# Small running maxima moved from SBUF into free columns of a PSUM bank, in a fused Perceiver block

## The chip, the core and the metric

The kernel runs on one core of one Trainium2 chip. The metric is the device time of one execution in microseconds (us), shown as the median of three runs. The engines are named as in the profile: PE is TensorE (matrix products), DVE is VectorE, ACT is ScalarE, POOL is GpSimd, SP is SyncE, which only issues DMAs here.

## What is computed

Three layers follow one another on `x` (8 batches, 128 rows, 512 columns), each with a residual add:

```
x = x + xattn(layernorm(x), ctx)   # 8 heads of 64, softmax over 2048 context rows of 384
x = x + attn(layernorm(x))         # causal mask, softmax over axis 1, 512 wide
x = x + ffn(layernorm(x))          # 512 -> 2048 -> 512, relu, hidden rounded to an 8-bit float
```

The change lies in the first layer, the cross attention. For each batch and head it is

```
q = xn @ Wq ; k = ctx @ Wk ; v = ctx @ Wv
attn = softmax(q k^T / 8)  over 2048 context rows
out  = (attn @ v) @ Wo + bo
```

## The kernel before

The cross attention is cut into `SLOTS = 128` slots: 8 batches, 4 quarters of the context (512 rows each), 4 pairs of heads. Slot `s` is head pair `p = s % 4` of unit `i = s // 4`; a unit is one quarter of one batch. Each matrix is kept as a high and a low half-precision part, and a product takes three passes. One step `s` of the pipeline does on PE: the values of slot s+1 into the PSUM bank `v_ps` (`value_tiles`), the keys of slot s into `k_ps` (`key_quarter`), the product of probabilities and values of slot s-5 into `o_ps[s % 2]` (`weighted_values`), and in even steps the scores of slots s-2 and s-1 into `e_ps[0]` and `e_ps[1]` (`scores`). So the work goes in pairs of steps.

The softmax is a running one over the four quarters of a batch. For each slot DVE reduces the scores to a negated maximum for each row and head (`quarter_maximum`). In quarter 0 this goes straight to `run`. In quarters 1 to 3 it goes to `q_max`, and a second instruction (L1535) takes the smaller of `q_max` and the `run` of the quarter before; that is the new `run`. ACT turns `run` into the bias of the exponential (`quarter_bias`, L1176) and computes the exponentials twice, as a half-precision part `p_h` (L1199) and in full as `p_f` (L1201). POOL subtracts the two for the low part `p_l` (L1981). SP turns both parts around by DMA transposes (L595, L598), and `weighted_values` reads them. `gaps` (L1543), once for each pair of slots in quarters 1 to 3, subtracts the old from the new `run`; ACT makes the factor `fade` from it (`fades_of`, L1185), by which DVE scales the accumulated output (`accumulate`, L1562). `GAPS` lists the even slots at which this happens, 48 of them.

Each engine runs its instructions in the order in which they are written, and waits on semaphores. The orders that matter here:

- DVE in an odd step s: the two maxima of slots s-3 and s-2, `accumulate` of slot s-6, the low part of the values of slot s+1 (`v_low`, L1517), `gaps`, the low part of the keys of slot s (`k_low`, L1521). In an even step: `accumulate`, `v_low`, `k_low`. In steps 111 to 126 a `weight_low` (L1580) stands ahead of `gaps`.
- ACT in an odd step: bias of slot s-3, first half of its exponentials, bias of slot s-2, the high part of the values of slot s+1 (`v_high`, L1164), second half of the exponentials, high part of the keys (`k_high`, L1170), `fades_of`.
- PE: `value_tiles` of the next slot waits until `v_low` has emptied `v_ps`, and `key_quarter` until `k_low` has emptied `k_ps`.
- POOL: `p_low` for each slot; once for each unit `ctx_low` (L1971), the low part of the next quarter of the context; late in the loop `weight_high` (L2040) and `add_bias` (L2025), for the later layers.

`weighted_values` fills columns 0 to 258 of its bank; the other columns of `o_ps[1]` are not used in the loop.

Of the kernel before, what the change touches and what calls it, by code (L numbers as in the profile page):

```python
# [4 lines left out]
F32 = mybir.dt.float32  # L5
# [3 lines left out]
ALU = mybir.AluOpType  # L9
ACT = mybir.ActivationFunctionType  # L10
AX = mybir.AxisListType.X

P = 128
# [3 lines left out]
PAIRS = HEADS // 2  # L17
QUARTERS = 4
# [40 lines left out]
def perceiver_kernel(nc, x, ctx_t, xwq, xwk, xwv, xwo, xbo, awq, abq, awk, abk, awv, abv,  # L59
# [6 lines left out]
        ("bq_col", [P, DCH], F32), ("bk_col", [P, DCH], F32), ("b1_col", [P, HC, 1], F32),  # L66
        ("b2_half", [P, D], F16),
        ("stats", [P, B, 6], F32), ("mean_var", [P, B, 2], F32), ("rstd", [P, B], F32), ("exponent", [P, B], F32),
        ("q_max", [P, 2, 2], F32), ("run", [P, 2, PAIRS, 2], F32), ("bias", [P, 2, PAIRS, 2], F32), ("gap", [P, 2, PAIRS, 2], F32),
        ("fade", [P, 2, PAIRS, 2], F32), ("acc", [P, PAIRS, 2, VW], F32), ("o_rec", [P, PAIRS, 2, 1], F32), ("o_sum", [P, 2, DH], F32),  # L70
        ("o_f", [P, 2, DH], F32),
        ("ones", [P, P], F32), ("bq_half", [P, DCH, 2], F16), ("bk_half", [P, DCH, 2], F16), ("bias_prod", [P, DCH], F32),
# [89 lines left out]
    assert t_halves_end <= halves_end  # L162

    (o_all, ident, causal, bo_row, bv_row, b2_row, bq_col, bk_col, b1_col, b2_half, stats, mean_var, rstd, exponent,
     q_max, run, bias, gap, fade, acc, o_rec, o_sum, o_f,
     ones, bq_half, bk_half, bias_prod, u_col, w_col, w_half, s_col, c_sum, c_col,
     shift) = keep.values()
    q_h, q_l = queries.values()
# [31 lines left out]
    with ExitStack() as ctx:  # L200
        def psum(name, shape):
            return ctx.enter_context(nc.psum_tensor(name, shape, F32))

        def sem(name):
            return ctx.enter_context(nc.semaphore(name))

        v_ps, k_ps = psum("v_ps", [P, 512]), psum("k_ps", [P, 512])
        e_ps = [psum("e_ps0", [P, 2, 512]), psum("e_ps1", [P, 2, 512])]
        o_ps = [psum("o_ps0", [P, 512]), psum("o_ps1", [P, 512])]

        kv_bank = [v_ps, k_ps]
        t_bank = [e_ps[0][:, 0, :], e_ps[0][:, 1, :], e_ps[1][:, 0, :], e_ps[1][:, 1, :]]
        r_bank = o_ps
        q_bank = [v_ps, o_ps[0], k_ps, o_ps[1]] + o_ps + o_ps

        const_ready = sem("const_ready")
# [36 lines left out]
        e_maxed = sem("e_maxed")  # L253
        bias_ready = sem("bias_ready")
        q_maxed = sem("q_maxed")
        gap_ready = sem("gap_ready")
# [86 lines left out]
        def unit_of(s):  # L343
            return s // PAIRS, s % PAIRS
# [49 lines left out]
        GAPS = [s for s in range(0, SLOTS, 2) if s // PAIRS % QUARTERS]  # L394

        def gaps_at(s):
            return GAPS.index(s)
# [275 lines left out]
        def _(pe):  # L673
# [78 lines left out]
            def weighted_values(s):  # L752

                i, p = unit_of(s)
                landed = 16 * (s // T_RING) + 16
                pe.wait_ge(pt_h_landed[s % T_RING], landed)
                pe.wait_ge(pt_l_landed[s % T_RING], landed)

                pe.wait_ge(v_split, PAIRS * i + PAIRS)
                if s >= 2:  # L760
                    pe.wait_ge(acc_ready, s - 1)
                elif s == 0:
                    pe.wait_ge(v_ones, 1)
                    pe.wait_ge(q_split, 8)
                acc_bank = o_ps[s % 2]
                for h in range(2):
                    at = h * VW
                    for j in range(JT):
                        pe.matmul(acc_bank[:, at:at + SUM_AT + 1], pt_h[:, s % T_RING, h * JT + j, :],  # L769
                                  v[:, i % V_RING, j, 2 * p + h, 0:SUM_AT + 1],  # L770
                                  start=(j == 0 and h == 0), stop=False, skip_group_check=True)
                        mm = pe.matmul(acc_bank[:, at + DH:at + SUM_AT + 1], pt_l[:, s % T_RING, h * JT + j, :],  # L772
                                       v[:, i % V_RING, j, 2 * p + h, DH:SUM_AT + 1],
                                       start=False, stop=(j == JT - 1), skip_group_check=True)
                mm.then_inc(pv_done, 1)
# [52 lines left out]
            def steady(s):  # L828

                if s + 1 < SLOTS:  # L830
                    value_tiles(s + 1)
                if s < SLOTS:
                    key_quarter(s)
                if 0 <= s - PV_LAG < SLOTS:
                    weighted_values(s - PV_LAG)
                if s % 2 == 0 and 2 <= s <= SLOTS:
                    scores(s - 2)
                    scores(s - 1)
# [199 lines left out]


            weighted_values(SLOTS - PV_LAG)  # L1040
            scores(SLOTS - 2)
            fold(0)
            scores(SLOTS - 1)
            project_out(0)
            for r in range(1, 4):
                weighted_values(SLOTS - PV_LAG + r)
                project_out(r)
# [54 lines left out]
        def _(act):  # L1102
# [76 lines left out]
            def fades_of(s):  # L1179

                i, p = unit_of(s)
                act.wait_ge(gap_ready, gaps_at(s) + 1)
                if i >= 2:
                    act.wait_ge(acc_ready, s - 2 * PAIRS + 2)
                act.activation(fade[:, i % 2, p:p + 2, :], gap[:, i % 2, p:p + 2, :], ACT.Exp, scale=EXP_SCALE)\  # L1185
                    .then_inc(fade_ready, 1)
# [190 lines left out]
            quarter_bias(SLOTS - 1)  # L1377
            exps(SLOTS - 1, 0)
            fades_of(SLOTS - 2)
            exps(SLOTS - 1, 1)  # L1380
            for r in range(3):
# [80 lines left out]
        def _(dve):  # L1462
# [60 lines left out]
            def quarter_maximum(s):  # L1523

                i, p = unit_of(s)
                dve.wait_ge(e_filled, s + 1)
                if i >= 2:
                    dve.wait_ge(bias_ready, s - 2 * PAIRS + 1)
                if i % QUARTERS == 0:
                    dve.tensor_reduce(run[:, i % 2, p, :], e_ps[s % 2][:, :, :], AX, ALU.max, negate=True).then_inc(e_maxed, 1)  # L1530
                    return
                dve.tensor_reduce(q_max[:, s % 2, :], e_ps[s % 2][:, :, :], AX, ALU.max, negate=True).then_inc(q_maxed, 1)  # L1532
                dve.wait_ge(q_maxed, PAIRS * (i - 1 - i // QUARTERS) + p + 1)
                dve.wait_ge(e_maxed, s - PAIRS + 1)
                dve.tensor_tensor(run[:, i % 2, p, :], q_max[:, s % 2, :], run[:, 1 - i % 2, p, :], ALU.min).then_inc(e_maxed, 1)  # L1535

            def gaps(s):

                i, p = unit_of(s)
                dve.wait_ge(e_maxed, s + 2)  # L1540
                if gaps_at(s) >= 4:
                    dve.wait_ge(fade_ready, gaps_at(s) - 3)
                dve.tensor_tensor(gap[:, i % 2, p:p + 2, :], run[:, i % 2, p:p + 2, :], run[:, 1 - i % 2, p:p + 2, :],  # L1543
                                  ALU.subtract).then_inc(gap_ready, 1)

            def accumulate(s):

# [591 lines left out]
```

## Time and profile before

| | |
|---|---|
| median of three runs | 966.65 us (965.09, 966.65, 969.07) |
| the profiled execution | 967.87 us, span from first to last instruction 965.8 us |
| PE | 912.1 us busy, 94% of the span |
| DVE | 642.5 us, 67% |
| ACT | 596.9 us, 62% |
| POOL | 508.6 us, 53% |
| chain that ended last | PE 71%, DVE 13%, ACT 7%, issue 3% |

The first columns say how long an engine worked, not what it held up. The chain is followed back from the last instruction, at each step to what released it. The slots take the time from about 40 to 770 us; what comes after is the two later layers, in which PE is busy too. A timeline row gives start, duration, engine, line, operation, output and inputs, and in brackets the idle time before it and what ended that; adjacent instructions of one kind can stand in one row (x3).

### The profile page before, as it was taken

Reading aid. Unit: us, or ns where it says so; the run is one execution under the profiler, and the core shown is the slowest. Engines: PE = TensorE matmul, PEld = TensorE weight load, DVE = VectorE, ACT = ScalarE, POOL = GpSimd, SP = SyncE. Lnnn points to the kernel's source line nnn. Section 1 sums busy time; section 2 is a strip of 40 time slices with the busy share of each in tenths; the row PEclk is TensorE's granted clock in tenths of the full one; section 3 lists DMA queues with packets and bytes.
Section 4 is the critical chain, followed back from the end, with each engine's and each line's share of the span. In section 5 each row is a group of like instructions: output and inputs, shape, how many; then the busy total and the mean of one; then the engine's idle time right before and its main releaser. Section 6 shows DMA issues by size and latency. Waiting matters only on the chain.

```text
span 965.8 us, 17868 instructions
## 1 busy us (share of the span) xinstructions
PE 912.1 (94%) x6354; PEld 459.8 (48%) x6354; DVE 642.5 (67%) x1085; ACT 596.9 (62%) x1126; POOL 508.6 (53%) x394
## 2 busy tenths in 40 slices
PE   7999999999989999999999999999898899999998
PEld 4444445444544544454445444444443455554444
DVE  6546665666666566656665666678777778886634
ACT  4757767767677766777677668666675712326540
POOL 2535566556645755565467556767796586310000
PEclk9999999999999999999999999999899999999999
DMA  9346766756656566655656766987888546134501
GB/s 327 77 88 120 124 131 153 151 120 127 137 121 126 134 139 128 126 137 134 133 142 134 134 130 137 185 198 143 174 148 170 110 68 140 26 108 88 168 19 76
DMA packets 340263, 126.24 MB, mean 131 GB/s; under 512 B 316113, under 2 KB 317905, under 8 KB 340177
## 3 DMA queue, kind: packets, MB, share of 16 engines
q1 hardware_dynamic: 324032, 94.30, 48.8%
q10 hardware_dynamic: 16144, 30.81, 10.4%
q8 instruction: 52, 0.85, 0.4%
q14 instruction: 35, 0.28, 0.1%
HBM read 45.36 MB, written 2.10 MB: 49 GB/s over the span
## 4 chain that ended last, share of the span: by engine, by line
PE 71%; DVE 13%; ACT 7%; issue 3%; POOL 1%; SPq 1%; DMA 1%; ACTq 0%; DVEq 0%; POOLq 0%
PE v_ps L679 21%; PE k_ps L679 20%; PE e_ps L748 7%; PE e_ps L679 7%; DVE run L1535 5%; PE o_ps L769 4%; DVE q_max L1532 4%; PE e_ps L1034 3%; PE o_ps L772 2%; ACT p_h L1199 2%; ACT v L1164 2%; PE o_ps L1027 2%; DVE v L1517 2%; PE e_ps L1027 1%; ACT p_f L1201 1%
## 5 line engine op out<-in xcount | busy, mean ns | idle before, releaser
L1981 POOL TENSOR_TENSOR p_l<-p_f,p_h 128x1024 f16<-128x1024 f32 x128 | 274.4, 2144 | 268.9 <-ACT p_f L1201 266.0
L1199 ACT ACTIVATE p_h<-e_ps,bias 128x512 f16<-128x512 f32 x256 | 176.7, 690 | 6.2 <-issue 4.0
L1201 ACT ACTIVATE p_f<-e_ps,bias 128x512 f32<-128x512 f32 x256 | 177.3, 693 | 0.0
L1521 DVE TENSOR_TENSOR k_l<-k_ps,k_h 128x512 f16<-128x512 f32 x128 | 88.4, 691 | 128.3 <-ACT k_h L1170 128.3
L1517 DVE TENSOR_TENSOR v<-v_ps,v 128x512 f16<-128x512 f32 x127 | 87.9, 692 | 100.7 <-ACT v L1164 100.5
L679 PE MATMUL v_ps<-wv_h,ctx_h 128*128 128x512 f16 (+1 forms) x384 | 103.0, 377 | 30.5 <-DVE v L1517 30.5
L1532 DVE TENSOR_REDUCE q_max<-e_ps 128x2 f32<-128x1024 f32 x96 | 117.2, 1221 | 7.8 <-PE e_ps L748 2.1
L1176 ACT ACTIVATE bias<-run 128x2 f32<-128x2 f32 x128 | 26.0, 203 | 150.6 <-DVE run L1535 127.7
L679 PE MATMUL k_ps<-ctx_h,wk_h 128*128 128x512 f16 x384 | 105.0, 383 | 9.0 <-DVE k_l L1521 8.7
L769 PE MATMUL o_ps<-v,pt_h 128*128 128x129 f16 x1024 | 106.8, 221 | 2.0 <-DMA pt_l<-p_l 2.0
L679 PE MATMUL k_ps<-ctx_h,wk_l 128*128 128x512 f16 x384 | 105.1, 383 | 0.0
L679 PE MATMUL k_ps<-ctx_l,wk_h 128*128 128x512 f16 x384 | 104.8, 382 | 0.0
L772 PE MATMUL o_ps<-v,pt_l 128*128 128x65 f16 x1024 | 103.4, 193 | 0.0
L1971 POOL TENSOR_TENSOR ctx_l<-raw,ctx_h 128x1536 f16<-128x1536 f32 x31 | 96.0, 3098 | 12.3 <-ACT ctx_h L1156 11.7
L679 PE MATMUL v_ps<-wv_l,ctx_h 128*128 128x512 f16 (+1 forms) x384 | 102.5, 376 | 0.0
L679 PE MATMUL v_ps<-wv_h,ctx_l 128*128 128x512 f16 (+1 forms) x384 | 102.5, 376 | 0.0
L769 PEld LDWEIGHTS o_ps<-v,pt_h 128*128 128x128 f16 x1024 | 92.3, 97 | 17.3 <-issue 2.6
L772 PEld LDWEIGHTS o_ps<-v,pt_l 128*128 128x128 f16 x1024 | 90.8, 98 | 15.1 <-issue 0.3
L1164 ACT ACTIVATE v<-v_ps 128x512 f16<-128x512 f32 x127 | 75.6, 596 | 32.3 <-PE v_ps L679 27.8
L1170 ACT ACTIVATE k_h<-k_ps 128x512 f16<-128x512 f32 x128 | 77.1, 603 | 14.9 <-PE k_ps L679 12.7
L1535 DVE TENSOR_TENSOR run<-q_max,run 128x2 f32<-128x2 f32 x96 | 65.6, 683 | 3.3
L679 PEld LDWEIGHTS v_ps<-wv_h,ctx_h 128*128 128x128 f16 x384 | 28.2, 97 | 75.4 <-issue 60.1
(311 smaller groups left out, 1363.2 us busy)
## 6 DMA issues: line engine op xcount, KB each, us to landing
raw<-in_ctx_t ACTq DMA_DIRECT2D x29, 768.0 KB, 5.1
w_raw<-in_w_t SPq DMA_DIRECT2D x32, 256.0 KB, 3.7
pt_h<-p_h SPq DMA_TRANSPOSE x128, 3.2
pt_l<-p_l SPq DMA_TRANSPOSE x128, 3.1
out<-xr SPq DMA_DIRECT2D x7, 256.0 KB, 2.0
x_in<-in_x SPq DMA_DIRECT2D x6, 256.0 KB, 9.4
raw<-in_ctx_t SPq DMA_DIRECT2D x2, 768.0 KB, 9.7
o_all<-in_x ACTq DMA_DIRECT2D x6, 256.0 KB, 4.5
```

The lines of the kernel that those rows point to most:

```text
L679: mm = pe.matmul(acc, a(c), m(c), start=(i == 0), stop=(i == len(todo) - 1))
L769: pe.matmul(acc_bank[:, at:at + SUM_AT + 1], pt_h[:, s % T_RING, h * JT + j, :], v[:, i % V_RING, j, 2 * p + h, 0:SUM_AT + 1], start=(j == ...
L772: mm = pe.matmul(acc_bank[:, at + DH:at + SUM_AT + 1], pt_l[:, s % T_RING, h * JT + j, :], v[:, i % V_RING, j, 2 * p + h, DH:SUM_AT + 1], ...
L1164: act.activation(v_high_part(s), v_source(s), ACT.Copy).then_inc(v_hi, 1)
L1199: act.activation(p_h[:, s % H_RING, h, :], e_ps[s % 2][:, h, :], ACT.Exp, scale=EXP_SCALE, bias=bias[:, i % 2, p, h:h + 1]).then_inc(p_hi, 1)
L1201: act.activation(p_f[:, s % F_RING, h, :], e_ps[s % 2][:, h, :], ACT.Exp, scale=EXP_SCALE, bias=bias[:, i % 2, p, h:h + 1]).then_inc(p_ful ...
L1517: dve.tensor_tensor(v_low_part(s), v_source(s), v_high_part(s), ALU.subtract).then_inc(v_split, 1)
L1521: dve.tensor_tensor(k_l[:, s % K_RING, :], k_ps[:, :], k_h[:, s % K_RING, :], ALU.subtract).then_inc(k_split, 1)
L1532: dve.tensor_reduce(q_max[:, s % 2, :], e_ps[s % 2][:, :, :], AX, ALU.max, negate=True).then_inc(q_maxed, 1)
L1535: dve.tensor_tensor(run[:, i % 2, p, :], q_max[:, s % 2, :], run[:, 1 - i % 2, p, :], ALU.min).then_inc(e_maxed, 1)
L1971: pool.tensor_tensor(ctx_l[:, i % 2, :, :], raw[:, i % 2, :, :], ctx_h[:, i % 2, :, :], ALU.subtract).then_inc(ctx_split, 1)
L1981: pool.tensor_tensor(p_l[:, s % L_RING, :, :], p_f[:, s % F_RING, :, :], p_h[:, s % H_RING, :, :], ALU.subtract).then_inc(p_split, 1)
```

## The change

`q_max` leaves SBUF. It now lies in columns 384 to 387 of the bank `o_ps[1]`: two columns for the even slot, two for the odd one. A new tile `least` lies in columns 388 to 391. The minimum L1535 now has one input in PSUM (the own maximum) and one in SBUF (`run`). `gaps` becomes two instructions: `least` is the smaller of both slots' own maxima (PSUM) and the old `run` (SBUF), and the gap is `least` (PSUM) minus the old `run` (SBUF). Before, both inputs of the gap were `run`, in SBUF. Since the columns lie in a bank that PE writes, `weighted_values` of the odd slots before a gap also waits for that gap. The lines of the changed kernel are numbered up to 7 higher.

```
-        ("q_max", [P, 2, 2], F32), ("run", ...
+        ("run", ...
...
+        q_max, least = o_ps[1][:, 384:388], o_ps[1][:, 388:392]
...
@@ weighted_values(s), PE
+                if s + 1 in GAPS:
+                    pe.wait_ge(gap_ready, 2 * gaps_at(s + 1) + 2)
...
@@ fades_of(s), ACT
-                act.wait_ge(gap_ready, gaps_at(s) + 1)
+                act.wait_ge(gap_ready, 2 * gaps_at(s) + 2)
...
@@ quarter_maximum(s), DVE
-                dve.tensor_reduce(q_max[:, s % 2, :], e_ps[s % 2][:, :, :], AX, ALU.max, negate=True).then_inc(q_maxed, 1)
-                dve.wait_ge(q_maxed, PAIRS * (i - 1 - i // QUARTERS) + p + 1)
+                own = q_max[:, 2 * (s % 2):2 * (s % 2) + 2]
+                dve.tensor_reduce(own, e_ps[s % 2][:, :, :], AX, ALU.max, negate=True).then_inc(q_maxed, 1)
+                dve.wait_ge(q_maxed, 2 * gaps_at(s - s % 2) + s % 2 + 1)
                 dve.wait_ge(e_maxed, s - PAIRS + 1)
-                dve.tensor_tensor(run[:, i % 2, p, :], q_max[:, s % 2, :], run[:, 1 - i % 2, p, :], ALU.min).then_inc(e_maxed, 1)
+                dve.tensor_tensor(run[:, i % 2, p, :], own, run[:, 1 - i % 2, p, :], ALU.min).then_inc(e_maxed, 1)
...
@@ gaps(s), DVE
-                dve.wait_ge(e_maxed, s + 2)
+                before = run[:, 1 - i % 2, p:p + 2, :].rearrange("p a h -> p (a h)")
+                dve.wait_ge(q_maxed, 2 * gaps_at(s) + 2)
+                dve.tensor_tensor(least, q_max, before, ALU.min).then_inc(gap_ready, 1)
+                dve.wait_ge(gap_ready, 2 * gaps_at(s) + 1)
                 if gaps_at(s) >= 4:
                     dve.wait_ge(fade_ready, gaps_at(s) - 3)
-                dve.tensor_tensor(gap[:, i % 2, p:p + 2, :], run[:, i % 2, p:p + 2, :], run[:, 1 - i % 2, p:p + 2, :],
-                                  ALU.subtract).then_inc(gap_ready, 1)
+                dve.tensor_tensor(gap[:, i % 2, p:p + 2, :].rearrange("p a h -> p (a h)"), least, before, ALU.subtract)\
+                    .then_inc(gap_ready, 1)
```

DVE, one odd step of quarter 1 (the maxima, the values, the gap, the keys), before:

```order
L1532 TENSOR_REDUCE q_max<-e_ps 128x2 [waits bias_ready,e_filled]
L1535 TENSOR_TENSOR run<-q_max,run 128x2 [waits e_maxed,q_maxed]
L1532 TENSOR_REDUCE q_max<-e_ps 128x2 [waits bias_ready,e_filled]
L1535 TENSOR_TENSOR run<-q_max,run 128x2 [waits e_maxed,q_maxed]
L1554 COPY acc<-o_ps 128x2x129 [waits o_ready,pv_done]
L1517 TENSOR_TENSOR v<-v_ps,v 128x8x64 [waits v_hi]
L1543 TENSOR_TENSOR gap<-run 128x4 [waits fade_ready,e_maxed]
L1521 TENSOR_TENSOR k_l<-k_ps,k_h 128x512 [waits k_hi]
```

The same step of DVE in the changed kernel (`o_ps<-e_ps` is the maximum written to its new place, `o_ps<-o_ps,run` is `least`):

```order
L1536 TENSOR_REDUCE o_ps<-e_ps 128x2 [waits bias_ready,e_filled]
L1539 TENSOR_TENSOR run<-o_ps,run 128x2 [waits e_maxed,q_maxed]
L1536 TENSOR_REDUCE o_ps<-e_ps 128x2 [waits bias_ready,e_filled]
L1539 TENSOR_TENSOR run<-o_ps,run 128x2 [waits e_maxed,q_maxed]
L1561 COPY acc<-o_ps 128x2x129 [waits o_ready,pv_done]
L1520 TENSOR_TENSOR v<-v_ps,v 128x8x64 [waits v_hi]
L1546 TENSOR_TENSOR o_ps<-o_ps,run 128x4 [waits q_maxed]
L1550 TENSOR_TENSOR gap<-o_ps,run 128x4 [waits fade_ready,gap_ready]
L1524 TENSOR_TENSOR k_l<-k_ps,k_h 128x512 [waits k_hi]
```

No instruction has moved past another; one is added ahead of the gap, 48 times in all.

PE, the even step after it (keys, then the first instruction of `weighted_values` into `o_ps[1]`), before:

```order
L679 MATMUL k_ps<-ctx_h,wk_h 128x512 [waits k_split,ctx_split]
L679 MATMUL k_ps<-ctx_h,wk_h 128x512 x2
L679 MATMUL k_ps<-ctx_h,wk_l 128x512 x3
L679 MATMUL k_ps<-ctx_l,wk_h 128x512 x3
L769 MATMUL o_ps<-v,pt_h 128x129 [waits v_split,acc_ready,pt_l_landed2,pt_h_landed2]
```

And in the changed kernel:

```order
L680 MATMUL k_ps<-ctx_h,wk_h 128x512 [waits k_split,ctx_split]
L680 MATMUL k_ps<-ctx_h,wk_h 128x512 x2
L680 MATMUL k_ps<-ctx_h,wk_l 128x512 x3
L680 MATMUL k_ps<-ctx_l,wk_h 128x512 x3
L772 MATMUL o_ps<-v,pt_h 128x129 [waits acc_ready,v_split,gap_ready,pt_l_landed2,pt_h_landed2]
```

The wait for `gap_ready` is new. `k_split` in the first row counts the `k_low` that follows this gap on DVE.

## Rows read from the trace of the kernel before

**Rows 1.** Busy time of the page (us, share of the span, instructions).

```profile
PE 912.1 (94%) x6354; PEld 459.8 (48%) x6354; DVE 642.5 (67%) x1085; ACT 596.9 (62%) x1126; POOL 508.6 (53%) x394
```

**Rows 2.** Waits, 80 to 608 us: engine, line, releaser: us, times, longest.

```profile
ACT bias L1176 <- DVE run L1535: 97.3, 35, 3.2
...
PE v_ps L679 <- DVE v L1517: 25.1, 18, 1.4
```

**Rows 3.** Windows, each one pair of slots: busy us by engine, clock, DMA share, GB/s.

```profile
384.31:394.99 10.68, 10.68 (x84) 5.45 (x82) 6.60 (x13) 7.39 (x17) 4.26 (x3) 1.00 0.79 161
394.99:407.21 12.22, 10.82 (x82) 5.46 (x81) 9.04 (x14) 8.65 (x17) 7.35 (x4) 1.00 0.43 96
```

**Rows 4.** Timeline of DVE in the first of these pairs.

```profile
385.18 1.22 DVE L1532 TENSOR_REDUCE q_max<-e_ps 128x2 f32<-128x1024 f32 x1
386.44 0.16 DVE L1535 TENSOR_TENSOR run<-q_max,run 128x2 f32<-128x2 f32 x1
...
388.75 0.69 DVE L1517 TENSOR_TENSOR v<-v_ps,v 128x512 f16<-128x512 f32 x1 [0.25 <-ACT v L1164]
...
390.44 0.69 DVE L1521 TENSOR_TENSOR k_l<-k_ps,k_h 128x512 f16<-128x512 f32 x1 [0.93 <-ACT k_h L1170]
```

**Rows 5.** Timeline of DVE in the second pair.

```profile
397.11 2.44 DVE L1535 TENSOR_TENSOR run<-q_max,run 128x2 f32<-128x2 f32 x1
...
401.70 0.69 DVE L1517 TENSOR_TENSOR v<-v_ps,v 128x512 f16<-128x512 f32 x1 [0.26 <-ACT v L1164]
```

**Rows 6.** Timeline of POOL in the second pair.

```profile
396.44 3.10 POOL L1971 TENSOR_TENSOR ctx_l<-raw,ctx_h 128x1536 f16<-128x1536 f32 x1
```

**Rows 7.** Timeline of PE, the next values in either pair.

```profile
390.31 0.81 PE L679 MATMUL v_ps<-wv_h,ctx_h 128*128 128x512 f16 x3
...
402.54 0.81 PE L679 MATMUL v_ps<-wv_h,ctx_h 128*128 128x512 f16 x3 [1.40 <-DVE v L1517]
```

**Rows 8.** Groups of DVE, 80 to 608 us: xcount, busy us, mean ns, idle before.

```profile
L1535 DVE TENSOR_TENSOR run<-q_max,run 128x2 f32<-128x2 f32 x70 | 52.4, 748 | 2.4
...
L1554 DVE COPY acc<-o_ps 128x258 f32<-128x258 f32 x22 | 9.3, 421 | 0.0
L1543 DVE TENSOR_TENSOR gap<-run 128x4 f32<-128x4 f32 x35 | 5.3, 152 | 0.0
```

**Rows 9.** Single lines, whole span: ns min/median/max, first and last start.

```profile
L1517 DVE TENSOR_TENSOR v<-v_ps,v x127: 684/692/693, 14.1 to 753.1; 128x512 f16<-128x512 f32 x127
```

```profile
L1562 DVE SCALAR_TENSOR_TENSOR acc<-acc,fade,o_ps x192: 334/342/352, 88.1 to 786.4; 128x129 f32<-128x129 f32 x192
```

**Rows 10.** Windows, late in the slots: columns as in Rows 3.

```profile
608.59:755.04 146.45, 133.87 (x962) 66.56 (x961) 109.80 (x163) 95.49 (x184) 108.76 (x70) 0.97 0.82 166
678.00:684.80 6.80, 5.78 (x29) 2.91 (x31) 3.54 (x8) 3.71 (x7) 3.21 (x3) 0.50 0.78 159
729.00:732.60 3.60, 3.19 (x8) 1.17 (x9) 2.06 (x5) 2.91 (x5) 0.45 (x1) 0.53 0.90 206
```

**Rows 11.** Timeline of DVE at the longest late wait.

```profile
673.05 3.23 DVE L1580 SCALAR_TENSOR_TENSOR av_l<-w_in,av_h 128x512 f16<-128x512 f32 x1
676.20 2.07 DVE L1543 TENSOR_TENSOR gap<-run 128x4 f32<-128x4 f32 x1
678.20 0.68 DVE L1521 TENSOR_TENSOR k_l<-k_ps,k_h 128x512 f16<-128x512 f32 x1
```

**Rows 12.** Timeline of POOL at the same place.

```profile
672.63 3.10 POOL L1971 TENSOR_TENSOR ctx_l<-raw,ctx_h 128x1536 f16<-128x1536 f32 x1
```

**Rows 13.** Timeline of PE, the two longest waits for the keys' bank.

```profile
679.02 1.44 PE L679 MATMUL k_ps<-ctx_h,wk_h 128*128 128x512 f16 x3 [3.64 <-DVE k_l L1521]
...
729.40 1.44 PE L679 MATMUL k_ps<-ctx_h,wk_h 128*128 128x512 f16 x3 [3.62 <-DVE k_l L1521]
```

**Rows 14.** Timeline of DVE, last gap of the slots.

```profile
768.20 1.92 DVE L1543 TENSOR_TENSOR gap<-run 128x4 f32<-128x4 f32 x1
```

**Rows 15.** Timeline of PE, first fold of weights after it.

```profile
770.87 1.02 PE L679 MATMUL v_ps<-wo_h,q_h 128*128 128x512 f16 x4 [1.21 <-DVE f_l L1668]
```

More of the change, by code:

```diff
@@ L68, in perceiver_kernel @@
         ("stats", [P, B, 6], F32), ("mean_var", [P, B, 2], F32), ("rstd", [P, B], F32), ("exponent", [P, B], F32),
-        ("q_max", [P, 2, 2], F32), ("run", [P, 2, PAIRS, 2], F32), ("bias", [P, 2, PAIRS, 2], F32), ("gap", [P, 2, PAIRS, 2], F32),
+        ("run", [P, 2, PAIRS, 2], F32), ("bias", [P, 2, PAIRS, 2], F32), ("gap", [P, 2, PAIRS, 2], F32),
         ("fade", [P, 2, PAIRS, 2], F32), ("acc", [P, PAIRS, 2, VW], F32), ("o_rec", [P, PAIRS, 2, 1], F32), ("o_sum", [P, 2, DH], F32),
@@ L164, in perceiver_kernel @@
     (o_all, ident, causal, bo_row, bv_row, b2_row, bq_col, bk_col, b1_col, b2_half, stats, mean_var, rstd, exponent,
-     q_max, run, bias, gap, fade, acc, o_rec, o_sum, o_f,
+     run, bias, gap, fade, acc, o_rec, o_sum, o_f,
      ones, bq_half, bk_half, bias_prod, u_col, w_col, w_half, s_col, c_sum, c_col,
```

## The prediction, made before the changed kernel ran

> **What bounds the kernel now.** I read the busy times first: PE works 94% of the span, some 54 of 965.8 us are left in which it does not [rows 1]. A change that touches no matrix product can win only there, so the next view is the waits, and of them those of PE. From 80 to 608 us PE has one kind of wait only: 18 times for `v_low`, 25.1 us in all, the longest 1.4 us, so all 18 are alike [rows 2]. ACT's 97.3 us of waiting for the running minimum L1535 in the same rows name a suspect, but an idle ACT costs nothing by itself.
>
> Next I cut windows at the starts of successive pairs of scores. A pair without such a wait takes 10.68 us and PE is busy in all of it; one with it takes 12.22 us [rows 3]. The starts of further pairs repeat these two lengths. So 10.67 is the floor that PE sets, and a disturbed pair costs 1.55 us more.
>
> The DVE timelines show where the two differ. In the clean pair the minimum takes 0.16 us [rows 4]. In the disturbed one it takes 2.44 us, for two numbers per partition [rows 5]; it began at 397.11 and ended at 399.55. POOL's `ctx_low` ran from 396.44 to 399.54 [rows 6]. The minimum lasted exactly until POOL was done. The group view says how often: 70 minima from 80 to 608 us take 52.4 us; at 0.16 us each they would take 11.2, so 41.2 us are excess, and 41.2 / 2.28 = 18, the count of PE's waits. The 35 gaps there have a mean of 152 ns: none is held [rows 8].
>
> What is held and what is not? `v_low` reads PSUM and SBUF and writes SBUF; its 127 executions span 684 to 693 ns. `accumulate`, with its large inputs in SBUF and PSUM, spans 334 to 352 ns over 192 [rows 9]. POOL is busy 53% of the time [rows 1], so many of these ran beside it, and none was ever late. The minimum and the gap have both inputs in SBUF, and so has `weight_low`, whose row shows 3.23 us [rows 11]. So what waits for POOL is a DVE instruction with two inputs in SBUF.
>
> How 2.28 us become 1.55: in the clean pair `v_low` ends at 389.44 and PE starts on `v_ps` at 390.31; in the disturbed one `v_low` ends at 402.39 and PE starts 0.15 us later [rows 4, 5, 7]. So a clean pair has 390.31 - 389.44 - 0.15 = 0.72 us of slack, and 2.28 - 0.72 = 1.56.
>
> **The change, part by part.**
>
> *The minima up to 608 us.* With the own maximum in PSUM they have the form of `v_low` and should not wait. 18 disturbed pairs become clean: 18 x 1.55 = 27.9 us.
>
> *What PSUM costs a small instruction.* No row shows DVE writing PSUM, or reading two numbers from it. Lower end: from the reduction of 1024 elements (1.22 us) and the copy of 258 (0.421 us) [rows 4, 8] each element costs (1.22 - 0.42) / 766 = 1.04 ns and a fixed part of 0.15 us is left, no more than a minimum takes today; so no loss. Upper end: a whole `accumulate`, 0.34 us [rows 9], so 0.18 us more per instruction. The near row in kind is the fitted fixed part, and I take 0.02 us more. Even the upper end, on the two reductions and two minima ahead of the second bias, is 4 x 0.18 = 0.72 us, just the slack. So it costs PE nothing at either end; if the cover were gone, the chosen value would cost 48 x 0.08 = 4 us and the upper end 35 us.
>
> The trace has nothing on this path that is dearer for lying in PSUM. Perfetto Trace Analysis, in its section Optimizing Scalar/DVE Operations, in the Trainium skill, speaks against the change: it gives about 125 ns of access overhead for DVE on PSUM against about 60 on SBUF. By that, four accesses on the path would add an estimated 0.26 us per pair, and the sum would still be the same, as that lies inside the slack; no run here shows the figure.
>
> *The added `least`.* One more instruction of 0.15 to 0.34 us ahead of `k_low` in 48 pairs. In the clean pair DVE idles 0.93 us before `k_low`, waiting for ACT [rows 4]; that covers it and the gap's own PSUM input. The fade becomes later by as much and is behind ACT's key copy. Cost nothing; uncovered it would be 48 x 0.2 = 10 us.
>
> *The new wait on PE.* `weighted_values` of an odd slot waits for a gap. But `key_quarter`, just ahead of it in the same step, already waits for the `k_low` that DVE does after that gap. The new wait is always met, except in the last steps, where there is no `key_quarter`. Queued behind it would be the scores. Its issue lies beside the nine products of the keys. I take zero; 0.05 us in each of 48 places would be 2.4 us.
>
> *608 to 755 us.* Twelve pairs take 146.45 us; at 10.67 they would take 128.0, so 18.4 are excess [rows 10]. Here POOL has the later layers' weights too and hits gaps as well. Two places are large. At the first `weight_low` waited for `ctx_low` (672.63 to 675.73) and ended at 676.28, then the gap took 2.07, and `k_low` came at 678.20 [rows 11, 12]; PE had waited 3.64 us [rows 13]. After it the granted clock is 0.50 for 6.8 us, in which 5.78 us of PE work are done, at the 1.2 GHz level where 2.4 is the other; half of that, 2.9 us, is loss [rows 10]. Behind the waits of 1.40 us three products still take 0.81 us, not 1.44 [rows 7, 13], so a short wait did not bring the clock down. The second place has 3.62 us and 3.19 / 2 = 1.6. Together 11.8 us; the other 6.6 us of the stretch belong to pairs with held minima and gaps.
>
> `weight_low` keeps both inputs in SBUF and stays held. Behind it `least` and gap take 0.35 us instead of 2.07, so `k_low` moves up by 1.7 us and the wait becomes 1.9 us. If POOL's work comes earlier too, because the pair before is no longer late, the wait is shorter still; I take 1.6 and no fall of the clock: 2 x 2.0 + 2.9 + 1.6 = 8.5 us. The other 6.6 us go. Sum 15.1, bounds 8 (waits of 2.4, clock falls anyway, a third of the small ones stays) and 18.4.
>
> *The end.* The last gap is held for 1.92 us [rows 14]; behind it stands `f_l`, for which PE waits 1.21 us [rows 15]. That goes: 1.2 us. Here the new wait on PE has no cover, but the gap should end at about 768.6, before PE is there. Bounds 0 and 1.9. After this PE has nearly no gaps, so what is won stays won.
>
> **Sum.** 27.9 + 15.1 + 1.2 = 44.2 us, against the profiled execution 967.87 - 44.2 = 923.7. The median of the runs is 1.2 us below that execution, so 922.5.
>
> **Rivals.** (a) *Only the regular part is won.* In the late stretch `weight_low` sits in the same queue, POOL's order against DVE changes, and both long waits stay with their slow clock: 27.9 + 6.6 + 1.2 = 35.7, 931 us. For it: `weight_low` is itself held for some 2.5 us (3.23 against the 0.68 of `k_low`, which has the same size) [rows 11]. Against: it was the gap that added the last 2 us.
>
> (b) *Small PSUM instructions are dear.* A write to PSUM and a dependent read right behind it cost 0.4 us more than I allow, in 48 pairs: 19 us back, 942 us. Against: the fitted 0.15 us; for it: no row shows such a write.
>
> (c) *All excess goes.* POOL is early enough that `weight_low` slips in ahead of `ctx_low`: 27.9 + 18.4 + 1.7 = 48, 918.6 us. SBUF — State Buffer in the Trainium skill, section SBUF: two separate sides, has the shared port pair held by whichever of the two starts first, for its whole instruction; by that this order would be possible, and no row shows it here.
>
> (d) *The change does not do what it says.* It is not the inputs that count, and a minimum that writes `run` in SBUF waits all the same: 966 us, within 0.5%. Against: `v_low` writes SBUF too and is never held.
>
> (e) *Slower.* As (d), and each held gap is now two held instructions. The lock goes to POOL in between, so the second waits for POOL's next operation, about 2 us. The gaps late in the slots stand right ahead of `k_low`, for which PE waits at the longest places; two of them longer by 2 us, with 3 us of slow clock, and the last one, 966.7 + 10 = 977 us. It decides as soon as a PSUM input does not free DVE. Against: [rows 9] again.
>
> **Chances.** Forecast 0.72, (a) 0.10, (b) 0.06, (c) 0.06, (d) 0.03, (e) 0.03. The likeliest case has bounds 27.9 + 8 + 0 and 27.9 + 18.4 + 1.9: 918 to 931 us. For 8 in 10 I add a part of (b): 917 to 934. Half a per cent is what a measurement of this kernel can tell from no change; faster by more than that: 0.94, within it 0.03, slower 0.03.
>
> **What would show it.** The minimum at 0.16 to 0.2 us with no long ones; no PE wait for `v_low` from 80 to 608 us, every pair 10.67 us; gap and `least` below 0.2 us each; `weight_low` still held; the granted clock 1.00 to 755 us. Minima of 2.4 us beside `ctx_low` would make the theory of the inputs wrong; pairs of 11 us without held instructions would make the slack wrong.

## The result and the profile after

The changed kernel takes 927.28 us (926.81, 927.28, 928.91) against 966.65 us before: a ratio of 0.9594, 95% interval 0.9557 to 0.9631. The profiled execution took 927.28 us with a span of 925.5, 40.3 us less than the span before. It lies in the predicted range (917 to 934), 4.8 us above the predicted 922.5.

The busy times of the changed kernel, to set beside [rows 1]:

```profile
PE 904.8 (98%) x6354; PEld 457.6 (49%) x6354; DVE 590.1 (64%) x1133; ACT 597.5 (65%) x1126; POOL 508.8 (55%) x394
```

DVE runs 48 instructions more and is busy 52 us less; what went was time in which it was held. The view of single lines says how evenly (ns min/median/max; L1536 is the own maximum, L1539 the minimum, L1546 `least`, L1550 the gap):

```profile
L1536 DVE TENSOR_REDUCE o_ps<-e_ps x96: 1221/1232/1233, 69.0 to 727.0; 128x2 f32<-128x1024 f32 x96
```

```profile
L1539 DVE TENSOR_TENSOR run<-o_ps,run x96: 158/159/160, 70.3 to 728.3; 128x2 f32<-128x2 f32 x96
```

```profile
L1546 DVE TENSOR_TENSOR o_ps<-o_ps,run x48: 156/159/165, 73.2 to 728.9; 128x4 f32<-128x4 f32 x48
```

```profile
L1550 DVE TENSOR_TENSOR gap<-o_ps,run x48: 160/162/164, 73.4 to 729.1; 128x4 f32<-128x4 f32 x48
```

No minimum is held any more, where the mean was 748 ns [rows 8]; 36 of the 96 still start beside a running `ctx_low`. And the small instructions are not dearer for PSUM: a minimum takes 159 ns instead of 161 (medians), the reduction that writes PSUM 1232 ns instead of 1221 (means). From the start of a maximum to the start of the minimum that reads it takes 1.27 us, and 1.26 before.

The pair that answers to the second window of [rows 3], in the changed kernel, with the late stretch of twelve pairs that answers to [rows 10] (windows: busy us by engine, granted clock, DMA share, GB/s):

```profile
377.58:388.25 10.67, 10.67 (x82) 5.44 (x82) 6.94 (x15) 8.71 (x17) 7.37 (x4) 1.00 0.58 113
580.31:716.62 136.31, 130.38 (x962) 65.72 (x961) 94.16 (x173) 95.65 (x184) 108.91 (x70) 0.99 0.94 179
```

DVE's and POOL's timelines in that pair, to set beside [rows 5, 6]:

```profile
379.71 0.16 DVE L1539 TENSOR_TENSOR run<-o_ps,run 128x2 f32<-128x2 f32 x1
...
382.02 0.69 DVE L1520 TENSOR_TENSOR v<-v_ps,v 128x512 f16<-128x512 f32 x1 [0.25 <-ACT v L1167]
382.63 0.16 DVE L1546 TENSOR_TENSOR o_ps<-o_ps,run 128x4 f32<-128x4 f32 x1
382.82 0.16 DVE L1550 TENSOR_TENSOR gap<-o_ps,run 128x4 f32<-128x4 f32 x1
```

```profile
379.04 3.10 POOL L1978 TENSOR_TENSOR ctx_l<-raw,ctx_h 128x1536 f16<-128x1536 f32 x1
```

The minimum starts 0.67 us into `ctx_low`, exactly as before, and is done while POOL still has 2.3 us to go. PE is busy in all of the pair's 10.67 us.

Where the 40.3 us of span came from, by the starts of the pairs in both timelines of PE: 0.3 before the slots, 28.0 from the first pair to the late stretch, 10.1 in the late stretch (146.45 to 136.31), 0.9 in the two short pairs behind it, 1.0 at the last gap and after.

PE's waits in the late stretch of the changed kernel:

```profile
PE o_ps L772 <- issue: 3.8, 3, 2.9
...
PE k_ps L680 <- DVE k_l L1524: 2.2, 2, 1.2
```

The wait for the keys' bank was foreseen. That of the output products was not: it was absent from the twelve late pairs before. It is put down to "issue", so the profile names no releaser; the first product waits for several semaphores at once, those of both halves of the probabilities among them. PE's rows at the place:

```profile
692.95 0.27 PE L772 MATMUL o_ps<-v,pt_h 128*128 128x129 f16 x1 [2.92 <-issue]
693.01 0.26 PE L775 MATMUL o_ps<-v,pt_l 128*128 128x65 f16 x1
```

The windows from that instruction on (columns as above):

```profile
692.95:694.00 1.05, 1.05 (x14) 1.05 (x15) 0.00 (x0) 0.00 (x0) 0.98 (x1) 0.50 1.69 140
694.00:696.00 2.00, 2.00 (x14) 0.77 (x13) 0.14 (x1) 0.00 (x0) 1.92 (x2) 0.50 1.10 240
```

After the wait of 2.92 us the granted clock is 0.50, the lower of its two levels (1.2 GHz), for some 3 us. And SP, in front of it:

```profile
681.26 1.38 SPq L580 DMA_TRANSPOSE q_h<-o_half  x1
682.68 1.27 SPq L580 DMA_TRANSPOSE q_l<-o_half  x1
683.99 2.03 SPq L585 DMA_TRANSPOSE ak_h<-wo_h  x1
686.06 1.27 SPq L585 DMA_TRANSPOSE ak_l<-wo_l  x1
687.43 1.26 SPq L596 DMA_TRANSPOSE pt_h<-p_h  x1
688.73 1.34 SPq L599 DMA_TRANSPOSE pt_l<-p_l  x1
```

SP issues without a break: two transposes of a batch's output, two of a weight, and only then those of the probabilities, for which PE waits.

### The profile page after: what moved, and what is told of

Its sections match the earlier page's. It is cut to its first block, busy times and chain, and to the rows that moved or that the text cites. A ratio compares the mean times of both kernels' runs of the same rounds, so it can differ in the third digit from the quotient of the medians.

```text
span 925.5 us, 17916 instructions
## 1 busy us (share of the span) xinstructions
PE 904.8 (98%) x6354; PEld 457.6 (49%) x6354; DVE 590.1 (64%) x1133; ACT 597.5 (65%) x1126; POOL 508.8 (55%) x394
## 3 DMA queue, kind: packets, MB, share of 16 engines
q1 hardware_dynamic: 324032, 94.30, 56.8%
q10 hardware_dynamic: 16144, 30.81, 10.5%
## 4 chain that ended last, share of the span: by engine, by line
PE 84%; POOL 4%; ACT 2%; DVE 2%; issue 2%; SPq 1%; DMA 1%; ACTq 0%; POOLq 0%; DVEq 0%
PE v_ps L680 25%; PE k_ps L680 24%; PE e_ps L749 9%; PE e_ps L680 7%; PE o_ps L772 6%; PE e_ps L1037 3%; PE o_ps L775 3%; PE o_ps L1030 2%; POOL p_l L1988 2%; PE e_ps L1030 1%; PE o_ps L791 1%; PE v_ps L1030 1%; SPq L623 1%; PE o_ps L970 1%; POOL wo_h L2047 1%
## 5 line engine op out<-in xcount | busy, mean ns | idle before, releaser
L1536 DVE TENSOR_REDUCE o_ps<-e_ps 128x2 f32<-128x1024 f32 x96 | 118.3, 1232 | 12.2 <-PE e_ps L749 6.2
L775 PEld LDWEIGHTS o_ps<-v,pt_l 128*128 128x128 f16 x1024 | 90.8, 98 | 14.6
L680 PEld LDWEIGHTS k_ps<-ctx_h,wk_h 128*128 128x128 f16 x384 | 37.3, 98 | 47.6 <-issue 3.5
L680 PEld LDWEIGHTS k_ps<-ctx_l,wk_h 128*128 128x128 f16 x384 | 37.6, 98 | 45.3
```

The source lines that it names most:

```text
L680: mm = pe.matmul(acc, a(c), m(c), start=(i == 0), stop=(i == len(todo) - 1))
L1536: dve.tensor_reduce(own, e_ps[s % 2][:, :, :], AX, ALU.max, negate=True).then_inc(q_maxed, 1)
```

## The experiments

All ratios are against runs of the kernel before on the same chip. "Late excess" is the length of the same twelve late pairs less 12 x 10.67 us, read from the one profiled execution of a run; before it was 18.4, in the changed kernel 8.3, and in a second execution of the changed kernel 9.6. Late excesses that differ by less than 1.5 us are therefore not told apart.

**Minima alone.** The gap is computed as before:

```
-                dve.tensor_tensor(least, q_max, before, ALU.min).then_inc(gap_ready, 1)
-                dve.tensor_tensor(gap[...], least, before, ALU.subtract).then_inc(gap_ready, 1)
+                dve.tensor_tensor(gap[...], run[:, i % 2, p:p + 2, :], run[:, 1 - i % 2, p:p + 2, :], ALU.subtract)
```

> The own maxima lie in PSUM as in the changed kernel, but the gap is computed as before, from two inputs in SBUF, and no least is made. My theory (a DVE instruction with two SBUF inputs waits for POOL, one with a PSUM input does not; the regular 18 pairs are held by a minimum, the gaps matter only late): every pair up to about 580 us is 10.67 us, all minima 0.16 us, gaps are still held late in the slots (up to 2.1 us each); time between the two kernels but near the changed one, 930 to 936 us. Rival (the added least and the PSUM input of the gap carry a good part of the gain): 945 us or more. Rival (the gaps do not matter at all): 927 us, as the changed kernel.

Measured 927.13 us, ratio 0.9589 (0.9571 to 0.9606), late excess 7.5. This is the same as the changed kernel, as the second rival had it, and 3 us below the range of my theory. So the gap's part of the change, with its added instruction, brings nothing on top of the minima. The gaps are held, as this line shows, up to 3.05 us:

```profile
L1547 DVE TENSOR_TENSOR gap<-run x48: 150/152/3054, 73.5 to 728.9; 128x4 f32<-128x4 f32 x48
```

The worst one starts at 640.06 beside `ctx_low`, where the changed kernel has `weight_low` held at 638.70. One held instruction has taken the place of another: PE waits 1.35 us for the keys there, and 1.22 in the changed kernel.

**Gap alone.** The new `run` is copied to PSUM, and the gap reads the copy; the minima stay in SBUF:

```
+                dve.tensor_copy(least, run[:, i % 2, p:p + 2, :]...).then_inc(gap_ready, 1)
+                dve.tensor_tensor(gap[...], least, run[:, 1 - i % 2, p:p + 2, :]..., ALU.subtract).then_inc(gap_ready, 1)
```

> The kernel before, but with the gap taken from a copy of the new run in PSUM (one more DVE instruction, a copy with one SBUF input) and the old run in SBUF; the minima keep two SBUF inputs. My theory: the 18 regular holds of 2.44 us stay, with 12.22 us pairs; late holds of gaps go; the copy with a single SBUF input is not held: 957 to 963 us. Rival (any SBUF input of DVE waits for POOL): the copy is held in place of the gap, 966 us or more.

Measured 955.66 us, ratio 0.9889 (0.9868 to 0.9909), 1.3 us below the range that I gave. The 18 regular holds and pairs of 12.22 us stay. The copy has its single input in SBUF and is not held, nor is the gap. Five of the 48 copies start beside a running `ctx_low` or `p_low`, with 1.7 to 3.0 us of it to go:

```profile
L1544 DVE COPY o_ps<-run x48: 151/155/160, 73.2 to 757.2; 128x4 f32<-128x4 f32 x48
```

```profile
L1538 DVE TENSOR_TENSOR run<-q_max,run x96: 160/161/2448, 70.3 to 756.5; 128x2 f32<-128x2 f32 x96
```

The late excess is 8.1. So late in the slots either half of the change wins some 10 us, and both together no more.

**The kernel before, POOL's piece cut.** The minima stay in SBUF; only the length of what they wait for changes:

```
-                pool.tensor_tensor(ctx_l[:, i % 2, :, :], raw[:, i % 2, :, :], ctx_h[:, i % 2, :, :], ALU.subtract)
+                for c in range(CC):
+                    ins = pool.tensor_tensor(ctx_l[:, i % 2, c, :], raw[:, i % 2, c, :], ctx_h[:, i % 2, c, :], ALU.subtract)
```

> The kernel before, with POOL's ctx_low cut into three instructions of a third each (about 1.05 us); the minima stay in SBUF. My theory (the hold lasts until the running POOL instruction ends, and a clean pair has 0.72 us of slack): the minimum starts 0.67 us into ctx_low, so it is held about 0.4 us instead of 2.3, which the slack covers: pairs of 10.67 us up to 600 us, 933 to 940 us in all. Rival (POOL keeps DVE out until its whole row of instructions is done): minima of 2.4 us stay, 966 us. Rival (slack smaller than 0.4 us): pairs between 10.7 and 11 us, 940 to 948 us.

Measured 941.48 us, ratio 0.9737 (0.9715 to 0.9759), late excess 12.6; 1.5 us outside my range. DVE and POOL in one such pair:

```profile
384.95 0.51 DVE L1535 TENSOR_TENSOR run<-q_max,run 128x2 f32<-128x2 f32 x1
385.38 1.21 DVE L1532 TENSOR_REDUCE q_max<-e_ps 128x2 f32<-128x1024 f32 x1
386.62 1.06 DVE L1535 TENSOR_TENSOR run<-q_max,run 128x2 f32<-128x2 f32 x1
```

```profile
384.28 3.38 POOL L1972 TENSOR_TENSOR ctx_l<-raw,ctx_h 128x512 f16<-128x512 f32 x3
```

The first minimum is held until the first third ends (384.28 + 1.13 = 385.41; it ends at 385.46), so a running POOL instruction, not a row of them, keeps DVE out. What I overlooked: DVE now gets to its second minimum while the last third runs, and that is held too. Together 0.35 + 0.90 = 1.25 us; less the slack of 0.72 this is 0.53, and the pairs are 11.12 us, 0.45 over the floor. The slack rule holds. The time and the pairs fall in the ranges of the rival of a smaller slack, but the second hold accounts for them without it.

How long a hold lasts depends on what POOL runs. Beside its instructions with two SBUF inputs, `ctx_low`, `p_low` and `add_bias`, every held minimum and gap of the kernel before ends with them, within 0.02 us. Beside `weight_high`, which has one input, it is another matter (kernel before; x2 are two instructions of 1.49 us):

```profile
669.59 0.54 DVE L1535 TENSOR_TENSOR run<-q_max,run 128x2 f32<-128x2 f32 x1
```

```profile
669.50 3.06 POOL L2040 TENSOR_SCALAR av_h<-w_in 128x512 f16<-128x512 f32 x2
```

This minimum ends 0.63 us into the first `weight_high`, with 0.86 us of it to go. All seven minima that are held beside a `weight_high` end at that point, and one that starts 0.61 us into it takes 0.16 us. The prediction, in its rival (c), had a hold last for the whole instruction; here it does not. Why it ends there was not found.

**The changed kernel, POOL's piece cut.** The same edit on the changed kernel.

> The changed kernel with POOL's ctx_low cut into three. My theory (the waits left late in the slots come from weight_low, two SBUF inputs, held by ctx_low or a weight_high): weight_low of 3.26 us at 638.7 becomes about 1.5, its pair loses most of its 1.4 us; 923 to 926 us. Rival (what is left late is the transposes behind SP's queue and the DMA): same as the changed kernel, 927 us, the 2.9 us wait of the output products stays. Rival (three short POOL instructions cost their starts, and the low part of the context comes later): slower by 1 to 3 us.

Measured 927.62 us, ratio 0.9603 (0.9574 to 0.9631). This is the rival's time, not mine. `weight_low` takes at most 1.64 us now and PE never waits for the keys in the late stretch, yet the late excess is 8.2. All of PE's waiting is for the output products:

```profile
PE o_ps L772 <- issue: 5.1, 2, 4.5
```

The second execution of the changed kernel, with nothing cut, waits as long for them (5.1 us, the longest 4.4) and 1.2 us for the keys. So this trace doesn't show that the cut moved the waiting to the output products; it shows that shorter holds of `weight_low` leave the excess where it was.

**`weight_low` with one input.** This version leaves out the subtraction, so that the low part of a weight is the scaled weight itself:

```
-                dve.scalar_tensor_tensor(lo, src, W_SCALE, hi, ALU.mult, ALU.subtract).then_inc(wx_split, 1)
+                dve.tensor_scalar(lo, src, W_SCALE, None, ALU.mult).then_inc(wx_split, 1)
```

> The changed kernel, but weight_low leaves out its subtraction: it scales the weight alone, one SBUF input instead of two (this part of the computation is left out, the later layers get wrong low parts). My theory (late in the slots PE waits because weight_low is held by POOL): all weight_low at 0.7 us, the late pairs lose most of their 8.3 us of excess, 920 to 923 us. Rival (the transposes and the DMA set the late pace): the 2.9 us wait for the output products stays and the time is 925 to 927 us.

Measured 924.73 us, ratio 0.9566 (0.9545 to 0.9588), late excess 5.8. The edit did not do what I meant: this instruction, with one SBUF input, is still held.

```profile
639.56 3.29 DVE L1587 TENSOR_SCALAR av_l<-w_in 128x512 f16<-128x512 f32 x1
...
646.02 0.42 DVE L1587 TENSOR_SCALAR av_l<-w_in 128x512 f16<-128x512 f32 x1
```

When free it takes 0.42 us for 512 elements, against 0.68 for the two-input form. Less the fixed 0.15 us that is an estimated 0.53 ns per element against 1.04, and this faster form is held as well. SBUF — State Buffer in the Trainium skill, section SBUF: two separate sides, names just these two kinds, two-port performance modes and two SBUF inputs; the traces agree, with 3.29 us for the one and 2.44 for the other. Small one-input instructions are of neither kind: the copy of the gap-alone version, which writes PSUM, is not held, and nor is the reciprocal of two numbers per partition, from SBUF to SBUF (in the kernel before 14 of them run beside a POOL instruction, at most 168 ns). So this run doesn't show what the holds of `weight_low` cost. Its time isn't told apart from that of the changed kernel either (0.9545 to 0.9588 against 0.9575 to 0.9601 in the second run of it below).

**A filler on DVE, short and long.** In the changed kernel, ahead of the first maximum of each of the 48 pairs; n is 192, then 448:

```
+                if s in GAPS:
+                    dve.tensor_reduce(fill[:, gaps_at(s), :], e_ps[0][:, :, 0:n], AX, ALU.max)
```

> The changed kernel with one extra reduction of 384 elements ahead of the first maximum of each of the 48 pairs in quarters 1 to 3, about 0.55 us, some 0.47 of it not overlapped. My theory (0.72 us of slack from the scores to v_low): pairs up to 580 us stay at 10.67 us, at most 2 us more late in the slots, 927 to 930 us. Rival (the slack is less than 0.4 us): every such pair is longer by 0.1 us or more, 932 us or more.

> The same with a reduction of 896 elements, about 1.09 us, some 1.0 of it not overlapped. My theory: each of the 48 pairs becomes longer by 1.0 - 0.72 = 0.3 us, so pairs of 10.95 us, 927.3 + 48 x 0.3 = 941 us. Rival (ACT, not DVE, sets when the values are ready, and the slack is over 1 us): 927 to 930 us. Rival (no slack at all): 48 x 1.0 more, 975 us.

Short: 926.43 us, ratio 0.9586 (0.9568 to 0.9603), as low as without it; the pairs up to the late stretch stay at 10.67 us. Long: 939.95 us, ratio 0.9725 (0.9708 to 0.9743), 1 us from the 941 of the theory. DVE in one pair with the long filler, and its window:

```profile
385.26 1.09 DVE L1537 TENSOR_REDUCE fill<-e_ps 128x2 f32<-128x896 f32 x1
386.26 1.22 DVE L1538 TENSOR_REDUCE o_ps<-e_ps 128x2 f32<-128x1024 f32 x1
```

```profile
384.39:395.34 10.95, 10.84 (x83) 5.49 (x82) 7.94 (x16) 8.66 (x17) 7.36 (x4) 1.00 0.73 119
```

The filler takes 1.00 us from start to start, and the pair grows by 0.28: a slack of 0.72 us, the number that the prediction read off two timelines.

**SP's queue.** In the changed kernel, first the output's transposes moved, then the weights' spread too, then `ctx_low` cut as well; and the changed kernel again as their base:

```
-        OUTPUT_BEHIND[116] = 6
+        OUTPUT_BEHIND[122] = 6
...
-        WEIGHT_BEHIND = {109: 0, 110: 1, 112: 2, 113: 3, 115: 4, 116: 5, 118: 6, 119: 7}
+        WEIGHT_BEHIND = {109: 0, 110: 1, 112: 2, 114: 3, 116: 4, 117: 5, 119: 6, 121: 7}
```

> The changed kernel with SP's two transposes of the sixth batch's output moved from behind slot 116 to behind slot 122. Theory (late in the slots SP's queue is full, a transpose issue takes 1.3 us and those of the probabilities wait behind those of weights and outputs; the 2.9 us wait of the output products at 692.95 is made by them): that wait becomes about 0.4 us or less, 924.5 to 925.5 us, and the granted clock stays 1.00. Rival (the landing of the transposes, slowed by the other DMAs, makes the wait): no change, 927 us. Rival (the two only move the wait elsewhere in the same stretch): 926 to 928 us.

> The same, with the transposes of the weights also spread so that no two adjacent slots late in the row carry them (behind slots 109, 110, 112, 114, 116, 117, 119, 121 instead of 109, 110, 112, 113, 115, 116, 118, 119). Theory (SP's queue is full): fewer waits of the output products, 922 to 925 us. Rival (the weights' buffers are then freed later, POOL's weight_high waits for them and holds DVE): 926 to 930 us.

> The same, with POOL's ctx_low cut into three as well. Theory (once SP's queue has room, what is left is weight_low held by ctx_low for up to 3.1 us; pieces of 1.1 us shorten that): 1 to 2 us less than the version without the cut. Rival (weight_low is not on the path that sets the end): the same time as without the cut.

> The changed kernel once more, as the base of the other three runs on the same chip: 926 to 929 us by every theory.

Measured 926.03 (ratio 0.9590, 0.9577 to 0.9603), 930.89 (0.9638, 0.9623 to 0.9653), 930.66 (0.9649, 0.9632 to 0.9666) and, the base, 925.85 us (0.9588, 0.9575 to 0.9601). None beats the base, and my theories for the first three, 924.5 to 925.5 us, 922 to 925 and a gain of the cut on top, all missed. The windows of the first show why:

```profile
580.45:712.68 132.23, 128.75 (x962) 64.95 (x961) 94.73 (x173) 95.66 (x184) 109.45 (x70) 1.00 0.93 183
712.68:725.11 12.43, 9.92 (x73) 4.82 (x71) 6.79 (x14) 6.94 (x16) 5.68 (x3) 0.86 0.85 140
```

The late excess falls to 4.2 us, with no wait of the output products above 0.9 us in it, and the two short pairs behind it, 9.53 us in the changed kernel, become 12.43: PE now waits 2.51 us for the last transposes, and the granted clock is 0.86 there. In the other two the late excess is 5.2 and 5.4, and those pairs take 14.6 and 15.8 us. With SP's order as it was the changed kernel has 8.3 and 9.6, and its versions with minima alone, with `ctx_low` cut, with the short filler and with less to load have 7.4 to 8.2; only the one-input `weight_low` comes near, with 5.8. So the order of SP's queue sets a part of the excess, by these single executions, and what is taken out in one place is given back where it is put.

With the weights spread, the rival's mechanism shows too. POOL's `weight_high` waits until the transposes have freed its buffer, and the next `p_low` stands behind it; SP issues no transpose from 709.84 to 713.59:

```profile
709.86 1.49 POOL L2047 TENSOR_SCALAR wo_h<-w_in 128x512 f16<-128x512 f32 x1 [4.01 <-DMA ak_l<-wo_l]
```

The base itself shows how loose the late stretch is. The same kernel waits 4.43 us at 659.45 in this execution instead of 2.92 at 692.95, behind one transpose whose issue alone took SP 4.37 us:

```profile
651.94 4.37 SPq L596 DMA_TRANSPOSE pt_h<-p_h  x1
```

**Less to load.** The changed kernel, 12 of the 16 weight loads cut to a quarter; three quarters of those weights are left out:

```
+                cols = slice(0, D if i < W_RING else P)
-                act.dma_start(w_in[:, k, :], ...)
+                act.dma_start(w_in[:, k, cols], ...)
```

> The changed kernel, but the last 12 of the 16 weight loads of the slots fetch a quarter of their columns (64 KB instead of 256 KB; three quarters of those weights are left out). SP's queue and every compute instruction stay as they are. Theory (late in the slots the 16 DMA engines are full, share 0.96, and the landing of the transposes sets the waits of the output products): 2.4 MB less to move is some 8 us less of DMA time in the stretch, its excess over pairs of 10.67 us falls from 8.3 to 3 to 6 us, 922 to 924 us. Rival (SP's queue is what is full): the same as the changed kernel, 926 to 927 us.

Measured 925.31 us, ratio 0.9575 (0.9556 to 0.9593), late excess 7.5. Its late window:

```profile
580.12:715.65 135.53, 130.32 (x963) 65.39 (x962) 94.72 (x173) 95.69 (x184) 108.94 (x70) 0.99 0.86 162
```

The DMA share falls from 0.94 to 0.86 and PE gains nothing that can be told apart, where my theory had an excess of 3 to 6 us. So the loads of the weights don't set the late pace. SP's own queue, with the transposes, is by far the larger load of the DMA engines (56.8% of the span of all 16 in the changed kernel, against 10.5% for ACT's, which loads the weights). It was left as it was, and this run says nothing of it.

## Why the prediction was right, and where it was off

**The regular part held in every step.** The minimum with a PSUM input is not held; 18 pairs of 12.22 us became 10.67; 27.9 us were forecast and 28.0 came. The premise, that many of the instructions with a PSUM input had run beside POOL, was taken from POOL's busy share; the trace of the kernel before bears it out: 11 `v_low` and 7 `accumulate` end within a running `ctx_low`, and 88 `accumulate` within a `p_low`, none of them longer for it. That it is POOL's running instruction that holds DVE was argued from two coinciding ends; the cut `ctx_low` shows it, since the holds shrank to the ends of the pieces. That two SBUF inputs are what matters for these small instructions is shown by the minima and gaps alone and in turn. The slack of 0.72 us is shown by the fillers.

**PSUM's price** was taken as 0.02 us per instruction, with an upper end of 0.18. It is -0.002 us for the minimum, 0.011 for the reduction, 0.010 for the gap. Rival (b) is out: a write to PSUM and the dependent read behind it cost 0.01 us more, not 0.4. Of the estimated 65 ns more per access on PSUM (125 less 60) that follow from the Trainium skill, Perfetto Trace Analysis, section Optimizing Scalar/DVE Operations, nothing is seen in these durations.

**`least` and PE's new wait** cost nothing, as forecast: the version without `least` has the same time. The cover named for the new wait holds in the slots. With the fillers, in the last steps, where I had said it has no cover, the profile names the gap as the releaser once in each, 0.87 and 1.40 us.

**The late stretch is the step that was mis-sized**: 15.1 us forecast, 10.1 measured. These 5.0 us are about the 4.8 between forecast and result; the other terms nearly cancel. Some 1.3 us were won beyond the forecast, before the slots and in the short pairs above all, and the median, 1.2 us below the profiled execution before, is that execution itself after. I took the 1.6 us that would remain at each of two places as the only remainder. Those are there, 2.2 us in all. What I did not see is what is late next once DVE is not: the output products, which wait 3.8 us in all for probabilities whose transposes stand in SP's queue behind those of weights and outputs. I had priced SP at nothing without reading its rows, and the same unbroken order stands in SP's timeline of the kernel before:

```profile
718.56 1.27 SPq L579 DMA_TRANSPOSE q_h<-o_half  x1
719.88 1.28 SPq L579 DMA_TRANSPOSE q_l<-o_half  x1
721.20 1.27 SPq L584 DMA_TRANSPOSE ak_h<-wo_h  x1
722.51 2.00 SPq L584 DMA_TRANSPOSE ak_l<-wo_l  x1
724.62 1.27 SPq L595 DMA_TRANSPOSE pt_h<-p_h  x1
```

There PE had been held for the keys, and didn't yet need the probabilities when they came; that is my reading of the two traces, and no run isolates it. Behind the late stretch the kernel before did wait for them, so the warning stood in its trace:

```profile
761.21 0.22 PE L769 MATMUL o_ps<-v,pt_h 128*128 128x129 f16 x1 [1.96 <-DMA pt_l<-p_l]
```

In the changed kernel the clock also fell once, behind the wait of 2.92 us, where I forecast 1.00 throughout. The result lies between the forecast and rival (a), 3.7 us below the latter: part of the late gain was lost, as (a) had it, but for another reason. That the time stayed inside the range owes something to the width given to this term (8 to 18.4 us).

**The credit was misplaced too.** I gave 8.5 of the late 15.1 us to the gap. The two halves of the change are not a sum there: each alone brings the late excess from 18.4 to about 8.

**The end**: 1.2 us forecast, 1.0 measured, and 0.9 more in the short pairs ahead of it, where the wait of 1.96 us just shown is 1.07 in the changed kernel.

**What stays open**: what exactly the remaining 8 us are made of. Shown is that they stay when `weight_low` is held less, when the gaps are held again, and when three quarters of most weight loads are gone; and that they move with the order of SP's queue but do not vanish. Whether the landing of the transposes or their issue weighs more was not separated. Why some issues of a transpose take 2 to 4.4 us instead of 1.3 was not found. An order of SP's queue that keeps both ends was not tried further.

## What to carry to other kernels

One engine's running instruction can hold up another engine's, and the victim can be the smallest instruction of the program: look for a minimum duration of 160 ns and a maximum of 2446 in one group, and lay the victim's end beside the other engine's. Here moving one of DVE's two inputs from SBUF to PSUM removed the stall; cutting POOL's instruction removed a part of it, and exposed the next one. Before adding up gains in a stretch that several engines load heavily, read the queue that issues its DMAs too: what is late next may sit there, and two edits that each win ten microseconds may share the same ten.

## What the runs showed of the hardware

- A minimum, difference or copy of 2 or 4 elements per partition takes DVE 150 to 165 ns when it is not held, whether its inputs are in SBUF or one is in PSUM, and whether it writes SBUF or PSUM.
- DVE with two SBUF inputs waits for the end of POOL's running instruction where that has two SBUF inputs itself: 2.44 us beside one of 3.10, 0.51 and 1.06 beside three of 1.13. Beside POOL's one-input `weight_high` of 1.49 us the minimum is let go 0.62 us into it.
- With one input in PSUM and one in SBUF DVE is not held: 36 minima beside `ctx_low`, at most 160 ns.
- A one-input instruction of 512 elements, float32 to float16, SBUF to SBUF, takes 0.42 us when free and is held as well, 3.29 us; a one-input copy of 4 elements from SBUF to PSUM is not (5 of 48 executions beside POOL's two-input instructions, at most 160 ns), and nor is a reciprocal of 2 elements in SBUF (at most 168 ns).
- The issue of a DMA transpose takes SP 1.24 us in the median. In the four traces looked at (before, changed, changed again, output later) 23 to 33 of the 336 issues take over 1.9 us, the longest 4.37.
